# Earlier and later: weight pieces re-timed beside the last batch, and a router norm that goes to another tile

## The reference

```python
x = x + attn(layernorm(x))            # linear "mixer": Q, K products, cumulative sums, gates, Wo
x = x + xattn(layernorm(x), ctx)      # 16 heads of 32, softmax over 750 context rows, Wo
x = x + ffn(layernorm(x))             # expert choice: 32 experts, each takes its top 8 tokens
# ffn: logits = x @ gate_w.T + gate_b;  probs = softmax over the TOKENS
#      vals, idx = top_k(probs, 8) per expert
#      merged = sum over the 8 tokens of vals * x[idx]           (one row per batch and expert)
#      o = gelu(merged @ w1 + b1) @ w2 + b2;  out[idx] += vals * o
```

## Time and profile before

| | us |
|---|---|
| median of three executions | 2227.69 |
| the profiled execution's own time | 2225.7 |
| its span (first to last instruction) | 2224.0 |
| outside the span | 1.7 |
| TensorE busy | 1838.5 (83%) |
| VectorE, ScalarE, GpSimd busy | 1012.0, 746.3, 824.1 |
| mean granted TensorE clock | 0.914 of full speed |

### The profile page before, as it was taken

One profiled execution on the slowest core, in us unless ns is written; L12 is line 12 of the kernel. 1 busy time (PEld: TensorE's weight loads), 2 busy tenths in 40 slices (PEclk: granted clock), 3 DMA queues, 4 the chain that ended last, 5 costly groups with the idle time before them and its releaser, 6 DMA issues. The chain is left out here.

```text
span 2224.0 us, 41403 instructions
## 1 busy us (share of the span) xinstructions
PE 1838.5 (83%) x12594; PEld 1205.0 (54%) x12594; DVE 1012.0 (46%) x2542; ACT 746.3 (34%) x1551; POOL 824.1 (37%) x591
## 2 busy tenths in 40 slices
PE   7789999999999999999999999976655556555644
PEld 5667777777777777777777777742211111111111
DVE  1355767657666667676576676642100000000003
ACT  3144445445445454454454544532100000000000
POOL 0255555655555556465655555542000000000000
PEclk9899999999999999999999999977977787778776
DMA  5324333333243243332432433373999999999996
GB/s 170 88 65 105 80 90 93 84 89 89 75 115 78 77 97 84 89 98 75 103 81 77 106 83 74 86 297 125 407 421 422 422 420 423 422 422 419 421 365 241
DMA packets 142370, 421.35 MB, mean 189 GB/s; under 512 B 32140, under 2 KB 78188, under 8 KB 117756
## 3 DMA queue, kind: packets, MB, share of 16 engines
q1 hardware_dynamic: 135580, 411.70, 54.3%
q10 hardware_dynamic: 5760, 8.15, 1.0%
q0 software_dynamic: 992, 1.02, 0.1%
HBM read 307.37 MB, written 17.14 MB: 146 GB/s over the span
## 5 line engine op out<-in xcount | busy, mean ns | idle before, releaser
L1168 DVE TENSOR_REDUCE maxes<-bank 112x1 f32<-112x376 f32 (+1 forms) x1024 | 510.7, 538 | 120.6 <-PE bank L1377 116.8
L970 ACT ACTIVATE probs<-bank 125x448 f32<-125x448 f32 x768 | 399.9, 548 | 149.6 <-PE bank L1399 148.5
L1399 PE MATMUL bank<-q_st,k_st 98*125 98x224 f32 x1536 | 334.6, 304 | 17.6 <-DMA q_st<-max_two 14.7
L848 POOL TENSOR_TENSOR psum_keys<-psum_keys,probs 125x896 f32<-125x896 f32 x127 | 266.9, 2101 | 212.3 <-ACT probs L970 202.9
L1791 PE MATMUL bank<-ring,hid_T 128*32 128x512 f32 x1024 | 177.1, 854 | 203.0 <-DMA ring<-in_L_ffn_w 198.1
L1377 PE MATMUL bank<-k_st,q_st 96*112 96x376 f32 (+1 forms) x1024 | 318.8, 357 | 24.4 <-DVE maxes L1168 20.9
L1399 PEld LDWEIGHTS bank<-q_st,k_st 98*125 98x125 f32 x1536 | 257.0, 190 | 70.9 <-issue 33.5
L1695 DVE TENSOR_TENSOR o_fin<-bank,b_row 16x512 f32<-16x512 f32 x32 | 21.7, 679 | 586.3 <-PE bank L1744 586.3
L851 POOL TENSOR_TENSOR psum_keys<-psum_keys,probs 125x896 f32<-125x896 f32 x127 | 266.9, 2101 | 10.0
L1624 POOL DMA_DIRECT2D o_rows<-o_fin x31 | 15.3, 494 | 596.7 <-DVE o_fin L1695 596.7
L1791 PEld LDWEIGHTS bank<-ring,hid_T 128*32 128x32 f32 x1024 | 44.9, 150 | 311.2 <-issue 305.7
(11 more groups left out here) (169 smaller groups left out, 2740.4 us busy)
## 6 DMA issues: line engine op xcount, KB each, us to landing
ring<-in_L_ffn_w SPq DMA_DIRECT2D x128, 2048.0 KB, 30.7
k_st<-k_hi SPq DMA_DIRECT2D x512, 93.8 KB, 2.1
k_st<-k_lo SPq DMA_DIRECT2D x256, 93.8 KB, 2.2
q_st<-q_hi SPq DMA_DIRECT2D x504, 28.0 KB, 1.8
ctx_nat<-in_ctx SPq DMA_DIRECT2D x16, 750.0 KB
x_in<-in_x SPq DMA_DIRECT2D x16, 448.0 KB, 3.9
out<-x SPq DMA_DIRECT2D x16, 448.0 KB, 3.1
out<-ring ACTq DMA_DIRECT2D x28, 256.0 KB, 3.0
```

Source lines behind the costliest of these rows:

```text
L848: nc.gpsimd.tensor_tensor(psum_keys[:], psum_keys[:], lo, ALU.add).then_inc(pool_chain, 1)
L970: nc.scalar.activation(probs[n % 2][:, j, :], bank[5 + u % 2][0:SK, 0:2 * T], ACT.Exp, scale=SCALE).then_inc(probs_ready, 1)
L1168: nc.vector.tensor_reduce(maxes[:, j, t, c:c + 1], score_bank(n)[0:TT, 0:SC[c + 1] - SC[c]], AX.X, ALU.max).then_inc(s_drained, 1)
L1399: last = nc.tensor.matmul(bank[5 + u % 2][0:SK, kk * T:(kk + 1) * T], k_st[slot][:, j, k * SK:(k + 1) * SK], q_st[slot][:, j, :], start=Tr ...
```

## The change

1. **last_batch_weights.** Piece 0 is asked for before the stack of head group 3 of batch 15, with no wait on scores_ready. The pieces 1 and 2 move from head group 0 to head group 1, 3 and 4 from 1 to 2, and 5 and the extra one from 2 to 3, in front of piece 6, which stays in head group 3. Piece 7 stays in the tail. (The words of the change speak of "one head group sooner"; by the order of SP's rows only piece 0 goes forward, and six pieces go back by one head group.)
2. **router_apply in the tail** writes the normed rows into x1 and waits for x1_kept_ready, not for x2_stored. The transposes and the merge of the tail read x1.
3. **rt0 and rt1 in the tail.** All four transposes of token half 0 stand first, behind a wait for the first of the two norm instructions; the four of half 1 follow behind the wait for the second.
4. **picks.** GpSimd's memset waits for tok_ready 2 (both first takes) and adder_ready (four small copies of VectorE).

```diff
                 def last_batch_weights(kt):
-                    if kt == 0:
-                        sp.wait_ge(x1_ready, 2 * B)
-                        first_weights([0])
+                    if kt == 1:
                         sp.wait_ge(v_ready, NK * B)
...
                         first_weights([1, 2])
-                    elif kt == 1:
+                    elif kt == 2:
...
                         first_weights([3, 4])
-                    elif kt == 2:
+                    elif kt == 3:
                         first_weights([5])
                         extra_weight()
-                    else:
                         first_weights([6])
...
+                        if kind == "last" and kt == 0:
+                            sp.wait_ge(x1_ready, 2 * B)
+                            first_weights([0])
                         if kt == 0:
                             stack(b, 3)
...
-                        if kind == "last":
+                        if kind == "last" and kt:
                             sp.wait_ge(scores_ready, (LAST * 4 + kt) * 12 + 1)
                             last_batch_weights(kt)
...
+                def router_apply(kind, b, n):
+                    if kind == "tail":
+                        act.wait_ge(x1_kept_ready, B)
+                        norm_apply(2, n, x2, x1, xr_ready)
+                        return
                     act.wait_ge(x2_stored, b * 16 + 16)
                     norm_apply(2, n, x2, xr, xr_ready)
...
+                            if kind == "tail" and i == 0:
+                                wait_out(pe, *before("rt1", kind, b))
+                                pe.wait_ge(xr_ready, bb * 2 + 1)
+                                for kd in range(KD):
+                                    ...
+                                    nc.tensor.transpose(tokens(ps2[:, cols], 0),
+                                                        x1[:, 0, kd * P:(kd + 1) * P],
+                                                        ident[0:TT, 0:TT])
                             pe.wait_ge(xr_ready, bb * 2 + 2)
...
+                                if kind == "tail" and t == 0:
+                                    continue
...
             def _(pool):
+                pool.wait_ge(tok_ready, 2)
+                pool.wait_ge(adder_ready, HC)
                 nc.gpsimd.memset(picks[:], 0.0).then_inc(cleared, 1)
```

More of the change, by code:

```diff
@@ L942, in attention_apply @@
                     norm_apply(1, n, x1, xh, xh_ready)
-                def router_apply(b, n):
+                def router_apply(kind, b, n):
[3 more added lines that the diff above has]
+                        return
                     act.wait_ge(x2_stored, b * 16 + 16)
@@ L999, in step @@
                             if job == "rt0":
-                                router_apply(b - 1, norm_no(2, kind, b))
+                                router_apply(kind, b - 1, norm_no(2, kind, b))
                             fill(job, kind, b)
@@ L1278, in fill @@
                     if job[:2] in ("xt", "yt", "rt"):
-                        src = xr if job[0] == "r" else xh
+                        src = x1 if kind == "tail" else xr if job[0] == "r" else xh
                         if job[:2] == "xt":
@@ L1284, in fill @@
                         else:
+                            if kind == "tail" and i == 0:
+                                wait_out(pe, *before("rt1", kind, b))
+                                pe.wait_ge(xr_ready, bb * 2 + 1)
+                                for kd in range(KD):
+                                    ps2 = bank_of(f"rt{kd // 2}", kind)
+                                    cols = slice(kd % 2 * T, (kd % 2 + 1) * T)
+                                    nc.tensor.transpose(tokens(ps2[:, cols], 0),
+                                                        x1[:, 0, kd * P:(kd + 1) * P],
+                                                        ident[0:TT, 0:TT])
                             pe.wait_ge(xr_ready, bb * 2 + 2)
@@ L1354, in fill @@
                         pe.wait_ge(wt_ready, bb * 2 + 2)
+                        rows = x1 if kind == "tail" else xr
                         for t in range(2):
@@ L1358, in fill @@
                                     ps[k * E:(k + 1) * E, 0:P], weight_T[:, t, :],
-                                    xr[:, t, :].rearrange("n (p k) -> n k p", k=KD)[:, k, :],
+                                    rows[:, t, :].rearrange("n (p k) -> n k p", k=KD)[:, k, :],
                                     start=(t == 0), stop=(t == 1))
```

## The result

| | before | after |
|---|---|---|
| median, us | 2227.69 (2222.74 to 2231.18, 5 runs) | 2210.54 (2209.41 to 2212.52, 5 runs) |
| profiled execution, us | 2225.7 | 2212.52 |
| its span, us | 2224.0 | 2210.8 |
| mean granted clock in it | 0.914 | 0.913 |

The ratio of after to before is 0.9922, with a 95% interval of 0.9903 to 0.9941: faster by 17 us, 13 to 22. Forecast were 2212 and a range of 2206 to 2219. The two profiled executions differ by 13.2 us only.

A forecast was written before the change was run, and what follows sets the result against it. Reading weights bounds the expert block, so the end hangs on the first expert's start. Gains of 6.8 + 3.4 + 3.0 + 0.4 + 1.1 = 14.7 us gave 2212 us, 8-in-10 range 2206 to 2219.

The forecast's parts named there:

- The shift goes to the end one for one: Expert block: whatever brings TensorE's first w1 product sooner shortens the whole kernel by the same time.
- Pieces 1 and 2 behind group 1's start: Last batch, before head group 1: max_two no longer waits behind the pieces; gain 6.8 us (6.2 to 7.3).
- Group 2's max_two: Last batch, before head group 2: pieces land before max_two is issued, so its wait falls to 1.89 us; gain 3.4 us.
- rival 2: Before head group 2: pieces 1 and 2 still outstanding, the second wait stays, 3.4 us lost; 2215.5 us, chance 0.18.
- The norm to x1: Tail: ScalarE's norm no longer waits for the store, only for GpSimd's last root operation; gain 3.0 us (2.8 to 3.1).
- the halves: Tail: half 0's transposes run beside the second norm instruction, so the second copy starts sooner; gain 0.4 us (0.2 to 0.6).
- picks: Before the first expert: first takes no longer run beside GpSimd's memset; gain 1.1 us (0.5 to 1.1).
- Cover of more than 10 us: cost nothing: Group 3 and tail: later pieces and the table late<-routed still land over 10 us before needed; cost zero.
- The clock at zero: Groups 1 and 2: TensorE's clock may stay up, range 0 to 5 us; taken as 0.
- Rival 1: Groups 1 and 2: TensorE's clock stays up, 3 to 5 us more gain; 2208 us, chance 0.20.
- Rival 3: Last batch: the pieces don't hold max_two, so only 4.5 us come; 2222 us, chance 0.09.
- Rival 4: Tail: postponed pieces make the table and take late, a loss of some 13 us; 2240 us, chance 0.03.

The follow-up runs named there:

- e1: Kernel before with only the new places of the weight pieces; tail, halves and memset as before: 2220.68 us, ratio 0.9961 to the kernel before.
- after_third: Changed kernel measured again without any edit, in a later session: 2214.13 us, ratio 0.9941 to the kernel before.
- e2: Changed kernel with the old places of the weight pieces; norm to x1, halves and memset's wait kept: 2222.26 us, ratio 0.9969 to the kernel before.
- e5: Changed kernel with one 2 MB piece asked for behind the stack in head group 0: 2219.65 us, one run.
- e4: Changed kernel with the store of batch 14 moved behind group 1's start: 2208.87 us, ratio 0.9909; again 2210.99 us, ratio 0.9932.
- e9: Changed kernel with pieces 0 and 1 ahead of group 0's last three stack DMAs, each as eight 256 KB DMAs: 2216.95 us, one run.
- e7: Changed kernel with the tail's transposes in the old order, norm still to x1: 2214.57 us, one run.
- e3: Changed kernel without the wait in front of GpSimd's memset: 2211.79 us, ratio 0.9923 to the kernel before.
- after_again: Changed kernel measured once more without any edit, in a later session: 2209.64 us, ratio 0.9923 to the kernel before.
- e6: Changed kernel with pieces 5, extra and 6 asked for only in the tail, ahead of piece 7: 2217.00 us, ratio 0.9957 to the kernel before.

## Why the prediction was right

**The shift goes to the end one for one.** Right as far as it can be seen: the first w1 product is 14.7 us nearer to the zero, and the stream behind it is as long as before within 0.8 us. In the two later profiles of the changed kernel it was 677.9 and 675.8 us long, 3.1 and 1.0 over the one profile of before, so "one for one" is shown to about 3 us.

**The sum of 14.7.** That the account gives the forecast's sum to the tenth is luck. Pieces 1 and 2 brought 1.0 us less than forecast, and group 1 was 0.5 longer; 0.9 in group 2, 0.2 in group 3 and 0.4 in the tail, none of them in the forecast, made it up. The two other profiles of the changed kernel give 17.5 and 13.1 us at the same place. The terms are right each by itself, to about 1 us, and that is what the prediction can claim.

**Pieces 1 and 2 behind group 1's start: 6.8 us.** Measured 5.8, outside its bounds of 6.2 to 7.3 (6.2 in e1, in after_third 6.4). Right in its mechanism: e1 has it alone, e2 has it undone, and e5 brings it back with one piece. What I had too small was the store that now stands in front: I took 0.6 us over the quiet 1.89, and 1.1 at most, from its bytes at 421 GB/s. It was 0.9 to 1.6 (2.82 to 3.44 us), and e4 takes it away. While the store ran, DMA moved 254 to 311 GB/s (1459.0 to 1460.5 us of the first profile), and what counts is not its transfer but its landing, 3.4 us after its issue.

**Group 2's max_two: 3.4 us.** Right, 3.4. Pieces 1 and 2 landed by 1474.8, and max_two was issued at 1475.92: a margin of 1.1 us where I had 1.3. The latency was 1.88 to 1.93 us in all eleven profiled executions in which pieces wait for group 1 (in e5 and e9 only piece 2 does). The premise of rival 2 was stricter than it had to be: in e4 piece 2 landed at 1477.0, after max_two had been issued at 1474.62, and the latency was 1.88 all the same. By then the pieces were nearly through (164 GB/s and falling from 1474.5 on).

**The norm to x1: 3.0 us, the halves 0.4, picks 1.1.** 3.0, 0.6 and 1.1 in idle time (2.10 to 1.01), the first by its releaser in the rows and by e2, the other two by e7 and e3, which undo them.

**"Cover of more than 10 us: cost nothing" for pieces 5, extra, 6 and 7.** This step was wrong as it stands. They cost 1.8 us of store latency in the tail (e1), which the norm's new target hides in the changed kernel. I looked at what the pieces and the table were needed for, and not at the stores that stood behind them in SP's queue. The cover was smaller too: the table landed at 1525.5 (I had before 1524) and the take began at 1534.9, 9.4 us later; the store of batch 15 landed at 1526.6. As the edits came together, the sum was right all the same.

**The clock at zero.** It did fall at group 1 in each trace of the changed kernel, and even in e4 after a wait of only 1.3 us; that what stands before 1459 us decides this, as I argued, is not shown. In group 2 I expected no gain, and two in three profiled executions of the changed kernel had little or none (groups 1 and 2 together 31.3 us before, 30.8 and 32.1), one had 2.9. Rival 1, the clock up in both groups, came in no trace; half of it, the clock up in group 2, came in one of three, so it is a part of the spread.

**The medians.** They gained 17.2 us, the profiled pair 13.2. Of the 4.0 between, 2.0 are the profile before, which lay that much under its median, and 2.0 the profile after, which lay that much over its own and had a mean clock of 0.913 where the other four had 0.917 and 0.918. That those four kept the clock in group 2 as after_again did is likely; they have no trace that shows it. In three sessions the medians gained 17.2, 18.5 and 13.5 us.

**Rival 3** (pieces do not hold max_two, 2222) is out by e1 and e5. **Rival 4** (late pieces, slower) needed what e6 did, three more pieces into the tail, and even then the kernel stayed 11 us under before.

## What to carry to other kernels

A prefetch has a second price beside its bandwidth: the small DMA that a compute engine waits for waits with it, here although another queue issues it. Put a large load behind the event that this small DMA releases, and also each store of some hundred KB that has time (in e4 the wait went; that the kernel gains by it isn't shown). And before a load is postponed, look at what is issued behind it on the same queue up to the block's end, in issue time as well as in landing time.

## What the runs showed of the hardware that I had not expected

- One 2 MB load, issued on SP's queue 0.13 us after a 7 KB DMA on ScalarE's queue and followed by a 448 KB store, delays the latter from 1.9 to 8.3 us; three such loads, issued 0.7 us before it to 0.4 us behind it, and the store delay it to 9.2 us only, and 16 loads of 256 KB to 5.3 us.
- A 448 KB store alone, issued 0.02 to 0.60 us ahead of the 7 KB DMA, holds it until the store itself lands, 3.3 to 3.4 us after the store's issue.
- SP's issue of a 448 KB store, behind four pieces of 2 MB and a 960 KB table in 512-byte rows, took 17.46 us, against 1.44 in the kernel before and 3.31 in the changed one at the same place.
- A 128 x 64 copy on VectorE takes 1.2 to 1.3 us while GpSimd's memset of 128 x 1536 runs, 0.225 us otherwise (the prediction had this from one trace; e3 shows it both ways).
- The same kernel loses TensorE's full clock once or twice in the same stretch, from one execution to the next (28.4 against 32.1 us for the same two head groups).
